# Attention block: value products of the fourth head group two key tiles at a time, projections reordered, the row constants turned in a projection bank

## The reference

```
h = relu(layernorm(x))                       # x: (16, 512, 512)
q, k, v = h @ Wq + bq, h @ Wk + bk, h @ Wv + bv
scores = q k^T / sqrt(32), -inf where adj == 0   # 16 heads per graph
attn = softmax(scores); out = (attn v) @ Wo + bo
return x + out
```

## Time and profile before

| | us |
|---|---|
| runs | 1604.37, 1606.54, 1607.43; median 1606.54 |
| the profiled execution | 1606.12 |
| its span in the trace | 1604.2 |
| TensorE busy | 1552.0 (97%) |
| VectorE busy | 1434.8 (89%) |
| ScalarE busy | 1430.2 (89%) |
| GpSimd busy | 754.6 (47%) |
| mean granted TensorE clock | 0.987 of full |

### The profile page before, as it was taken

One profiled execution on the slowest core, in us unless ns is written; L12 is line 12 of the kernel. 1 busy time (PEld: TensorE's weight loads), 2 busy tenths in 40 slices (PEclk: granted clock), 3 DMA queues, 4 the chain that ended last, 5 costly groups with the idle time before them and its releaser, 6 DMA issues.

```text
span 1604.2 us, 27422 instructions
## 1 busy us (share of the span) xinstructions
PE 1552.0 (97%) x7489; PEld 1040.9 (65%) x7489; DVE 1434.8 (89%) x3505; ACT 1430.2 (89%) x3433; POOL 754.6 (47%) x674
## 2 busy tenths in 40 slices
PE   7899999999999999999999999999999999999987
PEld 5566666666666666666666667666666666667643
DVE  7889998998989989999998989989998998988885
ACT  4899899999989899899999989999999999989984
POOL 3245445454354445445454454445445454454442
PEclk9799999999999999999999999999999999999988
DMA  7434443534344344443444444344443444344320
GB/s 232 119 104 105 125 112 100 141 95 136 100 131 115 91 141 108 123 113 99 135 101 131 106 132 113 93 136 112 123 113 101 137 100 134 98 116 105 94 81 27
DMA packets 154064, 183.63 MB, mean 114 GB/s; under 512 B 67748, under 2 KB 69808, under 8 KB 153904
## 3 DMA queue, kind: packets, MB, share of 16 engines
q1 hardware_dynamic: 149024, 179.76, 41.5%
q10 hardware_dynamic: 4888, 2.11, 0.6%
HBM read 54.79 MB, written 16.78 MB: 45 GB/s over the span
## 4 chain that ended last, share of the span: by engine, by line
PE 74%; ACT 8%; SPq 7%; DVE 4%; issue 4%; DMA 2%; ACTq 1%; DVEq 0%
PE psP L857 33%; PE ps L914 14%; PE psO L944 14%; PE ps L926 12%; SPq L283 5%; ACT ps L530 4%; ACT probs L586 2%; SPq L324 2%; DVE ps L688 1%; DMA q_stack<-part_lo 1%; ACTq L492 1%; DVE probs L702 1%; PE ps L871 1%; DMA v_sb<-in_L_gnn_Wv_dram 1%; ACT hT_hi L596 1%
## 5 line engine op out<-in xcount | busy, mean ns | idle before, releaser
L444 POOL TENSOR_TENSOR probs<-probs,keep_k 128x512 int32<-128x512 int32 x438 | 574.4, 1334 | 580.7 <-ACT probs L586 579.2
L688 DVE CUSTOM_DVE_ANT_0 ps<-ps,bias_q 128x512 f32<-128x512 f32 x1024 | 706.6, 694 | 131.7 <-PE ps L914 127.3
L530 ACT ACTIVATE ps<-ps,neg_max 128x512 f32<-128x512 f32 x1024 | 687.0, 671 | 72.8 <-DVE neg_max L688 57.0
L586 ACT ACTIVATE probs<-ps 128x512 f32<-128x512 f32 x1024 | 618.0, 604 | 52.8 <-PE ps L926 25.4
L914 PE MATMUL ps<-k_stack,q_stack 96*128 96x512 f32 x1024 | 440.3, 430 | 30.5 <-ACT ps L530 26.7
L926 PE MATMUL ps<-q_stack,k_stack 98*128 98x512 f32 x1024 | 414.8, 406 | 5.6 <-ACT probs L586 4.1
L702 DVE SCALAR_TENSOR_TENSOR probs<-turned,probs 128x512 f32<-128x512 bf16 x512 | 368.0, 719 | 4.7 <-ACT probs L586 4.3
L914 PEld LDWEIGHTS ps<-k_stack,q_stack 96*128 96x128 f32 x1024 | 193.7, 189 | 222.1 <-ACT ps L530 103.9
L944 PE MATMUL psO<-probs,v_sb 128*32 128x512 f32 x2048 | 255.1, 610 | 1.7 <-ACT probs L586 1.5
L926 PEld LDWEIGHTS ps<-q_stack,k_stack 98*128 98x128 f32 x1024 | 197.0, 192 | 50.3 <-ACT probs L586 18.9
L530 ACT ACTIVATION_READ_ACCUMULATOR ps<-ps,neg_max 128x1 f32 x1024 | 216.7, 212 | 0.0
(11 more groups left out here) (84 smaller groups left out, 1882.1 us busy)
## 6 DMA issues: line engine op xcount, KB each, us to landing
k_stack<-oT_hi SPq DMA_DIRECT2D x380, 64.0 KB, 2.0
q_stack<-y_tile SPq DMA_DIRECT2D x360, 64.0 KB, 2.0
x_tile<-in_x_dram SPq DMA_DIRECT2D x66, 256.0 KB, 3.0
y_tile<-in_x_dram SPq DMA_DIRECT2D x62, 256.0 KB, 2.9
out_dram<-y_tile SPq DMA_DIRECT2D x62, 256.0 KB, 2.0
turned<-in_adj_dram SPq DMA_DIRECT2D x61, 256.0 KB, 3.0
q_stack<-part_hi SPq DMA_DIRECT2D x240, 64.0 KB, 2.0
k_stack<-oT_lo SPq DMA_DIRECT2D x196, 64.0 KB, 2.0
```

The costliest lines, as they stand in the source:

```text
L444: nc.gpsimd.tensor_tensor(bits, bits, keep_k[:, kt // 2, :], ALU.mult).then_inc(gpsimd_masked, 1)
L530: nc.scalar.activation(item, item, ACT.Exp, scale=-1.0, bias=neg_max[:, g % 2, col:col + 1], accum_out=exp_sum[:, col:col + 1]).then_inc(e ...
L586: nc.scalar.activation(probs[:, (SLOTS * b + n) % P_RING, :], ps2[:, n % 2, :], ACT.Exp, scale=SCALE).then_inc(exp2_done, 1)
L688: nc.vector.tensor_tensor_reduce(bank1(k, ("s", u)), bank1(k, ("s", u)), bias_q[:, qt, :], -SCALE, 3.0e38, ALU.add, ALU.min, neg_max[:, g ...
```

## The change

The value products of the fourth group (key tiles 12 to 15) went out as 12 in slot 50, 13 and 14 in slot 58, 15 in slot 62; now 12 and 13 go in slot 54, 14 and 15 in slot 62. The projections T = 12 to 15 become q3, v2, v3, k3. With the new `PV_AT`, T = 12 and T = 14 are dealt 3, 3, 3, 3 and T = 13 and T = 15 are dealt 4, 4, 0, 4.

The c turns leave the ring. They are issued at the end of slots 6, 22, 38 and 54, behind the value products of the slot, into bank 0 of psP, which no projection uses in slots u with T odd. TensorE waits for that bank's previous tile to be taken out before the turn, and the next projection in that bank (T even) waits until VectorE has copied c. VectorE copies c at the start of the next slot (7, 23, 39, 55; before: 8, 24, 40, 56), ScalarE's queue issues the two DMAs in slots 8, 24, 40, 56 (before: one later). In step 16 the turns of groups 2 and 3 use psP bank 1 and ps1 bank 0, and the last output projection accumulates in psP 0, psP 1, ps1 1 and ps1 2.

```diff
-PV_AT = {6: (0, 1), 14: (2, 3), 22: (4, 5), 30: (6, 7), 38: (8, 9), 46: (10, 11), 50: (12,), 58: (13, 14), 62: (15,)}
+PV_AT = {6: (0, 1), 14: (2, 3), 22: (4, 5), 30: (6, 7), 38: (8, 9), 46: (10, 11), 54: (12, 13), 62: (14, 15)}
...
-            ("v", 2), ("q", 3), ("v", 3), ("k", 3)])
+            ("q", 3), ("v", 2), ("v", 3), ("k", 3)])
...
-TURNS = {1: [("h", 0, 0)], 5: [("h", 1, 0)], 8: [("c", 1, -1)], 10: [("h", 2, 0)], 13: [("h", 3, 0)],
-         24: [("c", 2, -1)], 40: [("c", 3, -1)], 56: [("c", 0, 0)]}
+TURNS = {1: [("h", 0, 0)], 5: [("h", 1, 0)], 6: [("c", 1, -1)], 10: [("h", 2, 0)], 13: [("h", 3, 0)],
+         22: [("c", 2, -1)], 38: [("c", 3, -1)], 54: [("c", 0, 0)]}
...
-    _c = [x for x in TURNS.get(_u, ()) if x[0] == "c"]
-    RING += _c + [("s", _u)] + [x for x in TURNS.get(_u, ()) if x not in _c]
+    RING += [("s", _u)] + [x for x in TURNS.get(_u, ()) if x[0] == "h"]
...
+            if item[0] == "c":
+                return {2: psP[:, 1, :], 3: ps1[:, 0, :]}.get(item[1], psP[:, 0, :]) if k == B else psP[:, 0, :]
...
-                    for kind, n, rel in turns(k, u - 1):
+                    for kind, n, rel in turns(k, u - 2):
                         if kind == "c":
                             load_c(k + rel, n)
...
-                    for kind, n, rel in turns(k, u):
+                    for kind, n, rel in turns(k, u - 1):
                         if kind == "c":
                             take_turn(k, kind, n, rel)
...
                     wait_tile_out(*((k, T - 2) if T >= 2 else (k - 1, T + 14)))
+                    if T % 2 == 0:
+                        pe.wait_ge(c_rows_done, turned_c[0])
...
                 else:
+                    if k == B and n == 3:
+                        pe.wait_ge(exp1_done, 64 * B)
+                    elif k == B and n == 2:
+                        pe.wait_ge(y_done, 4 * LAST)
+                    else:
+                        wait_tile_out(k, (4 * n + 14) % 16 - 2)
                     pe.wait_ge(c_lo_done, due(4 * b + n + 1))
+                    turned_c[0] = 4 * b + n + 1
...
                 if g == 0 and n < 2:
                     pe.wait_ge(y_done, 4 * LAST - 1 + n)
+                    pe.wait_ge(c_rows_done, turned_c[0])
...
-                    for kind, n, rel in turns(k, u):
-                        if kind == "c":
-                            turn(k, kind, n, rel)
                     b, n = pass1(k, u)
...
                     for kind, n, rel in turns(k, u):
-                        if kind != "c":
-                            turn(k, kind, n, rel)
+                        turn(k, kind, n, rel)
```

More of the change, by code:

```diff
@@ L156, in attention_block @@
         LAST = B - 1
-        last_turn_bank = (B * len(RING) + RING.index(("c", 3, -1))) % 3
-        last_out = [psP[:, 0, :], psP[:, 1, :]] + [ps1[:, i, :] for i in range(3) if i != last_turn_bank]
+        last_out = [psP[:, 0, :], psP[:, 1, :], ps1[:, 1, :], ps1[:, 2, :]]
         def x_view(b, t):
@@ L811, in wait_bank1 @@
                         continue
[L812 to L816, removed]
+                    pe.wait_ge(h_hi_done, due(4 * b + n + 1))
+                    pe.wait_ge(h_lo_done, due(4 * b + n + 1))
                     return
@@ L823, in three_products @@
                 return nc.tensor.matmul(acc, w_l, m_h, start=False, stop=(kt == NT - 1))
+            turned_c = [0]
             def project(k, u):
@@ L866, in turn @@
                 bank = bank1(k, (kind, n, rel))
-                wait_bank1(k, (kind, n, rel))
                 if kind == "h":
+                    wait_bank1(k, (kind, n, rel))
                     pe.wait_ge(norm_done, due(4 * b + n + 1))
```

## The result

The changed kernel takes 1586.69 us (median of four runs, 1585.1 to 1589.11) against 1606.99 for the kernel before in the same sittings: a ratio of 0.9876 (95% interval 0.9855 to 0.9896). 20.3 us are gone; 14.5 were forecast, and 1586.7 lies inside the range of 1582 to 1602. In a later sitting it took 1584.77 against 1606.23, 0.9865 (0.9843 to 0.9888).

The account below looks back on a forecast made before the run. TensorE, 97% busy, was taken as the bound in places, VectorE and ScalarE (89% each) limiting the gain. 0.34 + 0.91 - 0.55 + 0.2 = 0.90 us a step, 15 times 13.5, with the drain 14.5: 1592 us, range 1582 to 1602.

Parts of the forecast that it names:

- The difference between the windows: Slots 48-63 take 1.30 us more than slots 32-47; this, 15 times, is what there is to win: 19.5 us.
- Part 1: Fourth group on TensorE: merging value products, one pair for two single key tiles, wins 0.34 us a step.
- Part 2: Slots 55 and 56: c leaves the ring, so its stall for ScalarE goes, 0.91 us a step.
- c's price behind value products: Ends of slots 6, 22, 38, 54: a c turn costs 0 to 0.22 us, taken as 0.11, so moving is neutral.
- rival C: C's weight load stands exposed behind value products, 6.7 us of the gain lost: 1599 us, chance 0.07.
- Part 3: Slots 52 to 54: pass-2 matmuls wait for ScalarE's exponentials, 0.55 us a step given back.
- Part 4: Slots 0 to 3: VectorE is less behind at slot 0, 0.2 us gained; ring waits at slots 2 and 3 stay.
- The drain: Step 16, slot 44: c comes over a microsecond earlier for a wait of 1.33 us, 1 us gained.
- A: Rival: nothing is given back, the fourth group runs like the third: 1584 us, chance 0.16.
- B: Rival: VectorE and ScalarE hold most of the gain, 0.3 us a step is left: 1601 us, chance 0.13.
- D: Rival: slower, TensorE stops in front of c for a late VectorE, 0.5 us per turn: 1622 us, chance 0.06.
- E: Rival: value products don't come out paired, tile 13 waits for its masks, 5 us lost, chance 0.03.

Follow-up runs that it names:

- The split kernel: The changed kernel with key tile 12 alone in slot 50 and 13 alone in slot 54: 1581.58 us, timed again 1582.57 (ratio 0.9854).
- the c turns alone: The changed kernel with value products and projection order put back as before, only the c turns moved: 1602.3 us (ratio 0.9965).
- pairs and order alone: The kernel before with the paired value products and new projection order, c turns still in the ring: 1589.19 us (ratio 0.9883).
- one slot moved: The kernel before with key tile 13 in slot 54 and 14 in slot 62, old projection order, c in the ring: 1589.85 us (ratio 0.9896).
- again: Second profile of the unaltered changed kernel, from the later sitting: 1584.77 us (ratio 0.9865).
- c twice: The changed kernel with each c turn issued twice in a row into the same bank: 1592.91 us (one run).

## Why the prediction was right, and where it was not

**The difference between the windows as the size of the gain: right.** The third group's 22.90 us against 24.20 was the frame, and 0.71 to 0.73 us of it were won in slots 48-63, where the sum 0.34 + 0.91 - 0.55 said 0.70. That they agree hides three errors: in what merging is worth, in what removes the stall, and in what the 0.55 is made of.

**Part 1, merging is worth 0.34: the price is right, the worth is not.** The split kernel pays it and loses nothing. What the prediction took for two separate terms, 0.34 won and 0.55 given back, is largely one: TensorE faster through slots 48 to 52 only meets ScalarE sooner.

**Part 2, the ring's stall goes because the ring is left: the size is right, the reason is not.** With the c turns alone moved, 0.92 us went at slots 55 and 56 and 0.64 came back at slot 54 as a wait for VectorE. With value products in slot 54 alone the stall went with the turns still in the ring. The prediction put down to the ring what a late VectorE costs, and the kernel makes both changes at once. Once value products stand in slot 54, leaving the ring adds 0.05 to 0.27 us a step (pairs and order alone against the two profiles of the changed kernel), and the ratios 0.9883, 0.9876 and 0.9865, with intervals that overlap, don't show that it adds anything.

**c's price behind value products: the term was mis-sized.** Taken at 0.11 (neutral), it is about 0, the lower bound. That is some 0.1 for each of slots 6 to 8, 22 to 24 and 38 to 40. Slots 16-31 show it (0.06 to 0.11 less); elsewhere part is eaten, most plainly in slot 10 (1.57 to 1.69-1.75), and slots 32-47 end where they were. The Trainium skill's rule on weight loads (TensorE: Matmul & The Clock Gate, "The mechanism"), by which c's load would stand exposed and rival C would hold, is not borne out here: the first turn costs nothing measurable, and the second 0.13. The prediction's 0.11 leaned on both neighbours of c being 32 columns wide; only the value products ahead of it are, the score matmul behind it is 128 wide.

**Part 3, what is given back: right in mechanism, and in size partly by luck.** Slots 52 to 54 lose 0.57 (means of 5.83 us against 5.26), forecast 0.55; the replay's two starts on ScalarE came out within 0.02 us. Cutting the high part to a quarter gave slot 54 0.30 to 0.32 back, as the queue said. But the replay had 0.49 us of waiting, 0.15 in slot 53 and 0.34 in slot 54. The pass-2 matmuls of slots 52, 53 and 54 begin only 0.06, 0.02 and 0.22 us late (means), 0.30 together. What makes up the rest is something it didn't have: a matmul whose permission comes just in time still costs 0.1 us, three times.

**Part 4, slots 0 to 3: right direction, under-sized.** Forecast 0.2; slot 1 alone goes from 2.09 to 1.52, which is its work without a wait. The prediction said that the ring's waits at slots 2 and 3 stay. The one at slot 3 does, the one at slot 2 goes. Against the earlier trace rows, where slot 2 began after 0.29 us of idle time, it now begins 733.15 - 731.63 = 1.52 us after slot 1 with none:

```profile
731.63 0.39 PE L920 MATMUL ps<-k_stack,q_stack 96*128 96x512 f32 x1
...
733.15 0.48 PE L920 MATMUL ps<-k_stack,q_stack 96*128 96x512 f32 x1
...
734.84 0.47 PE L920 MATMUL ps<-k_stack,q_stack 96*128 96x512 f32 x1 [0.27 <-ACT ps L530]
```

Slot 10 takes back 0.12 to 0.18, slot 2 up to 0.10, and 0.34 to 0.53 is left over slots 0-15. The kernel with one slot moved has the same 1.52, that with the c turns alone has 2.14. So this gain, too, comes from where the value products stand, and not from the ring; that VectorE catches up in the long slots 54 and 62 is the likely way, not tested apart.

**Ends.** The sum counted 15 steps. The start and step 0 gain as well: slot 0 of step 1 comes at 62.1 us instead of 65.1 (62.9 again). Of this 1.06 are at slot 55, where the turn stalled step 0 too (2.28 to 1.22); the rest was not traced. The drain was to gain 1 us, since its pass 2 waited 1.33 us for the last c. In slot 44 of both new profiles TensorE stands idle for 0.29 us, so that wait gave back the 1 us. From slot 0 of step 16 to the end, before, after and again:

```profile
1512.80:1604.20 91.40, 76.72 (x323) 40.27 (x322) 66.60 (x141) 61.99 (x142) 34.83 (x26) 0.90 0.19 59
```

```profile
1493.30:1587.30 94.00, 80.93 (x323) 43.12 (x321) 68.97 (x141) 61.26 (x142) 34.87 (x26) 0.85 0.19 58
```

```profile
1490.70:1581.50 90.80, 76.88 (x323) 41.92 (x321) 68.89 (x141) 61.09 (x142) 35.13 (x26) 0.90 0.19 60
```

At the same mean clock of 0.90 the drain gains 0.6; at 0.85 it loses 2.6. In the first profile the clock stood at its lower level, 1.2 GHz, in slot 22, and the value products took 3.51 us instead of 1.92:

```profile
1525.38 3.51 PE L950 MATMUL psO<-probs,v_sb 128*32 128x512 f32 x16
```

Before the clock fell, TensorE stood idle 0.57 and 0.26 us in slots 18 and 19, with no projections of q, k and v left to fill them. So the sum of the profile is 3.0 (start and step 0) + 0.5 (step 1) + 16.0 (14 steps of 1.146) - 2.6 (drain) = 16.9, the difference of the spans; of the second profile it is 22.7 by the same count. The prediction's 14.5 missed the start's 2 to 3 us and 0.24 to 0.47 us a step for c and slots 0 to 3, and in the first profile a drain that lost what it was to win.

**The rivals.** A (nothing given back) is refuted by slots 52 to 54; its 1584 is near the measured time by other terms. B is refuted by the totals; C by slots 22 to 24 and by c twice; D stands in the run with the c turns alone (0.43 us of idle, 0.63 of slot length). In the first profile of the changed kernel TensorE stands idle in front of c for 0.54 us at slot 54 of step 0 and for 0.24 and 0.08 us at slot 38 of steps 2 and 3, and in no other step. E didn't occur.

**A term put at nothing that was not nothing.** The prediction counted nothing for ScalarE's two DMA issues coming a slot earlier. Most of them take 0.5 to 0.6 us as before, but some take far longer. Of the 128 issues, none takes over 0.95 us in the kernel before and one each with one slot moved and with pairs and order alone. It is 8 and 6 in the two profiles of the changed kernel and 6 with the c turns alone. In steps 2 to 15 every slot 10 of over 2.1 us and every slot 43 of 1.5 us follows such an issue, which holds ScalarE and then TensorE. Slot 10 of step 9, the longest with 2.60 us:

```profile
839.88 1.67 ACTq L492 DMA_DIRECT2D q_stack<-c_rows  x1
841.59 0.66 ACT L530 ACTIVATE ps<-ps,neg_max 128x512 f32<-128x512 f32 x1 [1.68 <-DVE neg_max L688]
```

```profile
843.58 0.50 PE L920 MATMUL ps<-k_stack,q_stack 96*128 96x512 f32 x1 [0.50 <-ACT ps L530]
```

The maximum that the second line names was ready at 841.04; ScalarE began as the issue ended. In the first profile three such steps make nearly all of the 0.18 us by which slot 10 grew. It is part of the reason why c's free place doesn't show in the totals. Why these issues take longer was not tested.

## To carry to other kernels

Three engines were over 85% busy here, and the place of the stall was not its cause. In such a kernel ask which engine is late there, and put the dominant engine's longest work that nobody waits for into the slot where the late one needs time. One line that moved value products by four slots was worth three quarters of this change. Removing the resource that the wait was written down to was worth a quarter by itself, and nothing that the totals show once the line had moved. Count issue time saved on the bound engine as won only if its inputs can come earlier; check with the same work split again.

## Of the hardware, not expected

- A matmul whose permission comes in the last moment costs 0.1 us without showing idle time: its weight load starts with it and not ahead of it, the matmul is shown with 0.50 instead of 0.40 us, and the next step takes 0.34 instead of 0.23 (712.01 above; its load had waited 0.30 us for ScalarE).
- One turn of 32 columns directly behind value products, which use the array in 32-column shapes, cost nothing in slots 22 to 24; a second one 0.13 us.
- Four 128-column turns in the same place cost their full 0.4 us.
- An issue of c's DMA on ScalarE's queue takes 0.5 to 0.6 us most of the time and 1.2 to 1.7 us now and then, and ScalarE computes nothing meanwhile (839.88 above).
